# A transformer block pair on one core: the second phase's projections computed as three float32r products in place of one float32 product

## The reference, cut to what matters

```python
def _layer(x, wqkv, qs, ksc, wo, lg, lb, w1, b1, w2, b2):
    h = shift_token(x)                 # half of the channels one token later
    q, k, v = split(h @ wqkv, 3)       # 8 heads of 64
    q = l2norm(q) * qs; k = l2norm(k) * ksc
    q, k = rotary_xpos(q, k)
    o = local_attention(q, k, v)       # windows of 128, own and previous
    x = x + o @ wo
    h = layernorm(shift_token(x)) * lg + lb
    a, g = split(h @ w1 + b1, 2)       # hidden width 682
    return x + (a * gelu(g)) @ w2 + b2
for l in range(2):
    x = _layer(x, wqkv[l], ..., w2[l], b2[l])
return layernorm(x0 + x)
```

## Time and profile before

| | |
|---|---|
| median of three runs | 5642.62 us (5640.09 to 5645.47) |
| the profiled execution, its own time | 5642.98 us |
| its span, first to last instruction | 5641.2 us |
| granted TensorE clock, mean | 0.992 of full speed |
| first phase, about | 0 to 2,700 us |
| second phase, about | 2,700 to 5,641 us |

### The profile page before, as it was taken

The page is one execution under the profiler, slowest core; times in us unless marked ns, Lnnn a source line. Parts: engine busy times, 40 slices in busy tenths (PEclk is TensorE's granted clock), DMA queues, the critical chain, the costliest instruction groups (busy, mean ns, idle before and its releaser), DMA issues.

```text
span 5641.2 us, 145376 instructions
## 1 busy us (share of the span) xinstructions
PE 5465.1 (97%) x57552; PEld 2666.8 (47%) x57552; DVE 4151.5 (74%) x10780; ACT 3453.4 (61%) x6979; POOL 970.1 (17%) x1933
## 2 busy tenths in 40 slices
PE   8999999999999999999799999999999999999998
PEld 3444444444444444533455555555555555555553
DVE  5888888787888888787566667666666777677774
ACT  4766667676666767666455555555556565555654
POOL 2222222232222223222000000000000001010100
PEclk9999999999999999999899999999999999999998
DMA  3333333233333333333100000000000000000000
GB/s 70 55 55 69 55 60 60 50 74 55 66 55 59 63 51 72 55 60 76 43 12 16 8 16 12 12 16 8 16 32 19 16 19 16 20 16 20 19 16 19
DMA packets 128518, 215.60 MB, mean 38 GB/s; under 512 B 40032, under 2 KB 40160, under 8 KB 127072
## 3 DMA queue, kind: packets, MB, share of 16 engines
q1 hardware_dynamic: 127840, 206.30, 18.1%
HBM read 45.73 MB, written 25.17 MB: 13 GB/s over the span
## 4 chain that ended last, share of the span: by engine, by line
PE 71%; ACT 11%; issue 10%; DVE 4%; POOL 3%; SPq 0%; DMA 0%; POOLq 0%; ACTq 0%; DVEq 0%
PE ps L573 22%; PE ps L698 14%; PE ps L819 10%; PE ps L1040 6%; PE ps L1003 5%; PE ps L904 3%; ACT pt L1257 3%; PE ps L896 3%; PE ps L921 3%; ACT gates L1455 1%; ACT sm L1374 1%; PE ps L1005 1%; PE ps L871 1%; PE ps L880 1%; POOL both L2119 1%
## 5 line engine op out<-in xcount | busy, mean ns | idle before, releaser
L1257 ACT ACTIVATE pt<-ps 128x1024 f32<-128x1024 f32 (+7 forms) x2048 | 1237.5, 654 | 616.2 <-PE ps L573 465.1
L698 PE MATMUL ps<-pt,va 128*32 128x512 f32 (+3 forms) x3072 | 1226.5, 487 | 20.0 <-POOL pt L2089 20.0
L698 PE MATMUL ps<-pt,ones 128*32 128x512 f32 (+3 forms) x6144 | 1236.4, 489 | 0.0
L698 PE MATMUL ps<-pt,vs 128*32 128x512 f32 (+3 forms) x3072 | 1230.1, 488 | 0.0
L1631 DVE CUSTOM_DVE_ANT_0 junk<-ps,causal 128x128 bf16<-128x128 f32 (+3 forms) x2048 | 977.8, 487 | 298.4 <-PE ps L573 282.1
L573 PE MATMUL ps<-kt,qt 96*32 96x512 bf16 (+3 forms) x12288 | 1018.6, 329 | 43.8 <-DVE mc L1631 22.7
L573 PE MATMUL ps<-qt,kt 98*32 98x512 bf16 (+3 forms) x12288 | 835.9, 328 | 21.9 <-ACT pt L1257 21.0
L1635 DVE TENSOR_REDUCE mc<-ps 128x1 f32<-128x512 f32 x1024 | 706.4, 690 | 158.7 <-PE ps L573 127.9
L2089 POOL TENSOR_SCALAR_AFFINE_SELECT pt<-pt 128x256 f32<-128x256 f32 x1024 | 466.8, 456 | 1892.2 <-ACT pt L1257 1890.4
L819 PE MATMUL ps<-wqkv,xs 128*128 128x512 f32 x1536 | 727.9, 603 | 0.0
L1374 ACT ACTIVATE sm<-sm,mxw 128x256 f32<-128x256 f32 (+1 forms) x1024 | 493.5, 484 | 241.0 <-DVE mxw L1800 239.6
(11 more groups left out here) (151 smaller groups left out, 8551.3 us busy)
## 6 DMA issues: line engine op xcount, KB each, us to landing
qt<-part SPq DMA_DIRECT2D x768, 64.0 KB, 2.4
kt<-part SPq DMA_DIRECT2D x768, 64.0 KB, 2.5
ya<-wy SPq DMA_DIRECT2D x128, 128.0 KB, 2.3
yb<-wy SPq DMA_DIRECT2D x128, 128.0 KB, 2.3
xs<-between_phases SPq DMA_DIRECT2D x32, 512.0 KB, 3.8
xt<-in_x SPq DMA_DIRECT2D x16, 512.0 KB, 5.6
between_phases<-z SPq DMA_DIRECT2D x16, 512.0 KB, 2.8
between_phases<-xo SPq DMA_DIRECT2D x16, 512.0 KB, 2.7
```

Of the source, the lines that this page charges most:

```text
L698: mmi = pe.matmul(ps[32 * q:32 * q + 32, 4 + half, lo - half * 512:hi - half * 512], w, probs(kb)[:, i, lo - first(kb):hi - first(kb)], st ...
L1257: act.activation(probs(kb)[:, i, kb * P - first(kb):1024 - first(kb)], ps[:, 2 * i:2 * i + 2, :].rearrange("p a q -> p (a q)")[:, kb * P:1 ...
```

## The change

Each float32 matmul of the second phase's projections (`project`, `attention_out`, `gate`, `hidden`, `ffn_out`) becomes three matmuls in the type float32r. For this each operand is split into a rounded part (a copy into a float32r tile) and the residue (operand less rounded part, also float32r): the products are rounded x rounded, rounded x residue and residue x rounded. Scores, transposes, weighing and the means stay float32.

Who splits: VectorE the six gated tiles (`split_hidden`, a copy and a subtraction each) and the first weights and half of x; GpSimd the weights otherwise (`split_w1`, `split_wo`, `split_w2`, `split_wqkv`, once a layer), the inputs (`split_x`, once a half), the heads (`split_heads`, once a window) and the residue of the normalised tile (`residue`, once a half); ScalarE writes the normalised tile's rounded part with one more pass per channel block in `scale_bias`.

To find room, residues lie in place over their operands, `xo` lies over `cn`, the gated tile over `gates`, `sqx` over the rounded gated tile, `ot` is halved to four windows, and sums of squares go in place into `sqf` and `sqx`. There is only one `wqkv` in memory: layer 2's is loaded and split at windows 62 and 63. The residual no longer reads `xs`; SP loads the same data once more into `xm` (`load_residual`).

```diff
+PRODUCTS = (((0, 0, 0, 0), (0, 0, 1, 1), (0, 1, 0, 2)), ((0, 1, 1, 3), (1, 0, 0, 4), (1, 0, 1, 5)))
+THREE = ((0, 0), (1, 0), (0, 1))
...
+            def load_residual(m):
+                lb, half = divmod(m, 2)
+                if m >= 2:
+                    sp.wait_ge(xo_done, done(2 * m - 2))
+                if m:
+                    sp.wait_ge(fc_done, done(2 * m))
+                    sp.wait_ge(xsum_done, done(m))
...
+                load_residual(2 * lb)
...
+                load_residual(2 * lb + 1)
+                if lb + 1 == nb:
+                    sp.wait_ge(qk_full, done(nb * WIN))
+                    fill_qkv(1, 0, 1024)
+                    sp.wait_ge(v_full, done(nb * WIN))
+                    fill_qkv(1, 1024, 1536)
...
-                return pe.matmul(ps[:, bank, :], xs[:, kc, at:at + P], wqkv[l][:, kc, n * 512:n * 512 + 512],
-                                 start=kc == 0, stop=kc == 1)
+                for x, y, kc, k in PRODUCTS[part_of]:
+                    at = w * P + 1 - kc
+                    mmi = pe.matmul(ps[:, bank, :], (xsh, xsl)[x][:, kc, at:at + P], (wh, wl)[y][:, kc, n * 512:n * 512 + 512],
+                                    start=k == 0, stop=k == 5)
...
-                    pe.wait_ge(o_read, done(4 * m + 4))
+                    pe.wait_ge(otl_done, done(4 * m + 4))
...
+            def normed(m, n, to, tile, width, parts):
+                for part_of in parts:
+                    if n == 0 and part_of == 1:
+                        pe.wait_ge(cnl_done, done(2 * m + 2))
+                    for x, y, kc, k in PRODUCTS[part_of]:
+                        mmi = pe.matmul(to, (w1h, w1l)[y][:, kc, tile, 0:width], (cnh, cnl)[x][:, kc, :],
+                                        start=k == 0, stop=k == 5)
...
-                    pe.wait_ge(hn_done, done(2 * m + 2))
+                    pe.wait_ge(cnh_done, done(2 * m + 2))
...
+                    if oc == 0:
+                        pe.wait_ge(hhl_done, done(m * HB + j + 1))
+                    for k, (x, y) in enumerate(THREE):
+                        mmi = pe.matmul(ps[:, fbank(m, 19 + oc), :], (w2h, w2l)[x][rows, j, oc * P:(oc + 1) * P],
+                                        (hhh, hhl)[y][rows, j, :], start=j == 0 and k == 0, stop=j == HB - 1 and k == 2)
...
                 for kc in range(2):
+                    act.activation(cnh[:, kc, :], cn[:, kc, :], ACT.Identity,
+                                   scale=lnp[:, 0, kc:kc + 1], bias=lnp[:, 1, kc:kc + 1]).then_inc(cnh_done, 1)
                     act.activation(cn[:, kc, :], cn[:, kc, :], ACT.Identity,
...
-                dve.tensor_tensor(xm[:, oc, at], ps[:, fbank(m, 1 + oc), :], xs[:, oc, at], ALU.add).then_inc(xm_done, 1)
+                dve.tensor_tensor(xm[:, oc, at], ps[:, fbank(m, 1 + oc), :], xm[:, oc, at], ALU.add).then_inc(xm_done, 1)
...
+            def split_hidden(m, j):
+                dve.wait_ge(hh_done, done(m * HB + j + 1))
+                dve.tensor_copy(hhh[rows, j, :], gb_[rows, j, :]).then_inc(hhh_done, 1)
+                dve.wait_ge(hhh_done, done(m * HB + j + 1))
+                dve.tensor_tensor(hhl[rows, j, :], gb_[rows, j, :], hhh[rows, j, :], ALU.subtract).then_inc(hhl_done, 1)
...
                     gated(m, 1)
+                    split_hidden(m, 0)
                     gated(m, 2)
+                    split_hidden(m, 1)
                     normalise(W, 2)
                     normalise(W, 3)
                     combine(W + 1)
                     gated(m, 3)
+                    split_hidden(m, 2)
                     gated(m, 4)
                     heads_out(W)
+                    split_hidden(m, 3)
                     gated(m, 5)
+                    split_hidden(m, 4)
+                    split_hidden(m, 5)
...
+            def split_heads(W):
+                cols = slice(W % 4 * P, (W % 4 + 1) * P)
+                pool.wait_ge(o_read, done(W + 1))
+                pool.tensor_copy(oth[:, :, cols], ot[:, :, cols]).then_inc(oth_done, 1)
+                pool.wait_ge(oth_done, done(W + 1))
+                pool.tensor_tensor(otl[:, :, cols], ot[:, :, cols], oth[:, :, cols], ALU.subtract).then_inc(otl_done, 1)
...
+                if c == 0:
+                    combine(W + 1)
+                    final_channels(m - 1)
+                    if m >= 0:
+                        sum_channels(m)
+                        sum_squares(m)
+                    split_heads(W)
+                elif c == 1:
+                    residue(m)
+                    combine(W + 1)
+                    split_x(W // WIN + W % WIN // 4, 1 - W % WIN // 4)
+                    final_sum_squares(m - 1)
+                    split_heads(W)
...
+                if W % (4 * FIRST) == 3:
+                    split_wo(W // (4 * FIRST))
+                    split_w1(W // (4 * FIRST))
+                if W % (4 * FIRST) == 6:
+                    split_w2(W // (4 * FIRST))
+                if W == 4 * FIRST - 2:
+                    split_wqkv(1, 0, 1024)
+                if W == 4 * FIRST - 1:
+                    split_wqkv(2, 1024, 1536)
```

More of the change, by code:

```diff
@@ L8 @@
 BF16 = mybir.dt.bfloat16
+F32R = mybir.dt.float32r
 ALU = mybir.AluOpType
@@ L153, in sb, with over @@
             top[0] = at + n
+            place[name] = at
             return nc.alloc_sbuf_tensor_at(name, shape, dt, offset=at)
+        def over(name, other, shape, dt):
+            return nc.alloc_sbuf_tensor_at(name, shape, dt, offset=place[other])
         def sem(name):
@@ L316, in program @@
         stored = [sem(f"stored{h}") for h in range(2)]
-        wq_ready = [sem(f"wq_ready{l}") for l in range(LAYERS)]
+        wq_ready = sem("wq_ready")
         wo_ready = sem("wo_ready")
@@ L953, in mean @@
                 pe.wait_ge(xsum_done, done(m + 1))
-                pe.matmul(ps[:, fbank(m, 3), :], mean_w[:], both[:, 0, :], start=True, stop=True).then_inc(fm_full, 1)
+                pe.matmul(ps[:, fbank(m, 3), :], mean_w[:], both[:], start=True, stop=True).then_inc(fm_full, 1)
             def variance(m):
@@ L961, in variance @@
                 pe.wait_ge(ssum_done, done(m + 1))
-                pe.matmul(ps[:, fbank(m, 4), :], mean_w[:], both[:, 1, :], start=True, stop=True).then_inc(fv_full, 1)
+                pe.matmul(ps[:, fbank(m, 4), :], mean_w[:], sqf[:, 0, :], start=True, stop=True).then_inc(fv_full, 1)
             def final_mean(m, W):
@@ L2134, in final_sum_squares, with split_w1 @@
                 pool.wait_ge(lvar_full, done(n))
-                pool.tensor_tensor(bothf[:, 1, :], sqx[:, 0, :], sqx[:, 1, :], ALU.add).then_inc(lqc_sum, 1)
+                pool.tensor_tensor(sqx[:, 0, :], sqx[:, 0, :], sqx[:, 1, :], ALU.add).then_inc(lqc_sum, 1)
+            def split_w1(l):
+                pool.wait_ge(w1_ready, sent(l + 1))
+                for kc in range(2):
+                    pool.tensor_copy(w1h[:, kc, :, :], w1[:, kc, :, :]).then_inc(w1h_done, 1)
+                for kc in range(2):
+                    pool.wait_ge(w1h_done, done(2 * l + kc + 1))
+                    pool.tensor_tensor(w1l[:, kc, :, :], w1[:, kc, :, :], w1h[:, kc, :, :], ALU.subtract).then_inc(w1l_done, 1)
@@ new lines, in residue @@
+            def residue(m):
+                if m < 0:
+                    return
+                for kc in range(2):
+                    pool.wait_ge(cnh_done, done(2 * m + kc + 1))
+                    pool.wait_ge(hn_done, done(2 * m + kc + 1))
+                    pool.tensor_tensor(cnl[:, kc, :], cn[:, kc, :], cnh[:, kc, :], ALU.subtract).then_inc(cnl_done, 1)
+            def split_heads(W):
[4 more added lines that the diff above has]
+                pool.tensor_tensor(otl[:, :, cols], ot[:, :, cols], oth[:, :, cols], ALU.subtract).then_inc(otl_done, 1)
@@ new lines, in attend @@
+            def attend(W):
+                m, c = half_of(W), W % 4
+                if c == 0:
[11 more added lines that the diff above has]
+                    split_heads(W)
+                elif c == 2:
+                    combine(W + 1)
+                    split_heads(W)
+                else:
+                    combine(W + 1)
+                    split_heads(W)
```

228 lines of the change are left out of this document (148 added, 80 removed).

## The result

The changed kernel takes 5787.69 us (median; 5642.88 before in the same session), a ratio of 1.0258, 95% interval 1.0242 to 1.0274: 144.8 us slower. The profiled execution's span is 5787.4 us. The forecast was 5704 with a range of 5550 to 5830: the sign was right, the size less than half.

A forecast was written before the change was run, and what follows sets the result against it. PE was taken as the bound by a small margin only, over a 71.10 us VectorE and ScalarE loop in each 89.60 us half. The sum was 5643 + 40 (halves) + 21 (once only) = 5704 us, range 5550 to 5830.

The forecast's parts named there:

- The sum's 40 us for the halves: Second phase, collisions included: +0.7 us a half in layer 1, +1.8 in layer 2, 16 halves each.
- 21 once-only us: Layer 2 weight splits (+6, +4.5 each at windows 4 and 68, +5), between phases +3, end -2: +21 us.
- Two signs: Second phase: PE would be below 85% busy and VectorE busier than 80% if the forecast was right.
- The windows without disturbance: Four windows of a half without collisions: c = 0 -1.43, c = 1 -0.9 and +1.15, c = 2 -0.67, c = 3 -2.0 and +2.95.
- the two terms -2.0 and +2.95: Window c = 3: faster PE products save 2.0 us; `largest`, delayed by VectorE's split tail in c = 2, adds 2.95.
- the 1.1 us more for layer 2: Layer 2: VectorE's final add and normalise lie in its loop, no longer covered by PE time; +1.1 us a half.
- a smaller thing is left out of the sum: PE idles some 4 us in c = 3; lower clock for keys and values could cost 1.5 us a half, 48 us.
- Collisions: GpSimd's `split_heads` against VectorE's split tail at the end of c = 2: between 0 and 2.1 us, taken 1.0.
- Collisions everywhere: Rival: 5.1 of GpSimd's 15 us a half obstruct VectorE, in place of 1.6, +3.5 x 32: 5816 us; 14%.
- The tail is swallowed: Rival: VectorE's tail after combine in c = 2 stays within 4.2 us, no collision: 5557 us; 22% up to no change.
- PE stays bound: Rival: PE remains the bound, needing the 71 us loop to shrink by 11: 5190 us; 5%.
- The products are no faster: Rival: float32r products take 0.43 us each, PE becomes the bound with +28.3 us a half: 6549 us; 4%.

The follow-up runs named there:

- experiment 5: On the change: first, unread extra products in c = 1 and c = 3, 5742.6 us; second, these (fewer in c = 3) with GpSimd's c = 2 head split held back, 5695.7 us.
- experiment 6: Against the 5695.7 us kernel: loads and splits of layer 2's four large weights left out, so layer 2 uses layer 1's; 5672.4 us, ratio 1.0055.
- both fillers: The change plus 18 unread products in the wait of c = 3 and four and four in c = 1; 5742.6 us, ratio 1.0179.
- all three edits: The change plus unread products in c = 1 (four and four) and c = 3 (12), and GpSimd's c = 2 head split held back; 5695.7 us, ratio 1.0100.
- experiment 1: The change plus 18 unread key products before TensorE's wait for the maxima in c = 3; 5756.0 us, ratio 1.0202.
- experiments 4, 7 and 8: On the change: VectorE's splits 2 to 5 moved into c = 3, 5726.0 us; ScalarE rounding those tiles, residues and head split moved, 5650.2; last feed-forward product float32, 5621.3.

## Why the prediction was right or wrong

The 144.8 us, as the runs split them, beside the terms of the sum:

| part | measured, us | from | in the sum, us |
|---|---|---|---|
| halves without collision in c = 2 and at full clock | 7 | experiment 5: 16 x 0.2 + 16 x 0.25 | 8 |
| lower clock | 45 | experiment 5, first | 0 (upper end 48) |
| head split beside the tail of c = 2 | 47 | experiment 5, second | 32 |
| layer switch | 23 | experiment 6 | 13 |
| start (windows 0 to 7) and end of the phase | 23 | remainder | 8 |

(The sum's 40 us for the halves held 1.0 x 32 of the tail's collisions; of its 21 once-only us I count 6, 4.5 and 2.5 to the switch.) The edits also change the switch: window 63 takes 32.8 us in the change, 35.9 with both fillers and 38.1 with all three edits. So the parts are good to some 5 us, and the clock and the head split are, if anything, priced too low.

**What bounds the kernel: right.** TensorE became faster and turned that into waiting, first in front of the scores of c = 3 and at the gate, as written. Products at 0.232 us and not 0.215 cost PE 66 x 3 x 0.017 = 3.4 us a half, so it got 10.8 of its 14.2 us; the difference is hidden in those waits. Two signs were set too far: PE is 89% busy (below 85 written), VectorE 76 and 79% (above 80).

**The windows without disturbance: near, and in sum with luck.** c = 0 takes 18.55 us (forecast 18.65), c = 2 21.54 (21.6), c = 1 24.65 where its clock stays up (24.31, or 24.9 with its collision). c = 3 takes 26.08 at full clock and 24.70 without the collision as well (24.14, or 25.15 with a collision of 1.0). The gate's parts began 10.30 and 12.33 us into c = 1 (10.5 and 12.55). The copy of a split took 0.42 us (0.43), its subtraction 0.69; without the collision `largest` comes 7.22 us after `combine` (7.15 written, though the terms listed for it add up to 7.24).

But c = 1 started from 24.06, where 23.78 is typical: it lost 0.87 us, not 0.25, or 0.85 with its collision. c = 3 lost 1.51 (0.95); no run took the lag alone out of it, so how the two terms -2.0 and +2.95 share that miss is open. And the 1.1 us more for layer 2 did not come. Without the tail's collision the sum had -0.3 us a half in layer 1 and +0.8 in layer 2; measured are +0.2 and +0.25. That 7 us stand beside 8 is two errors of 8 and 9 us which cancel.

**The step that failed** is the last one, "a smaller thing is left out of the sum". Its working was right: PE idles in c = 3, keys and values run at the lower level, up to 1.5 us a half, 48 us; measured 45. That the two are so near is partly chance: c = 3 lost 1.8 us in layer 1 and 1.4 in layer 2 (experiment 1), and it was not only c = 3, since behind the two waits at the gate, 1.03 and 1.09 us, c = 1 lost 1.1 us too in every second half of layer 1. Nothing in the rows spoke for leaving it out, and the earlier trace rows showed the fall after 2.00 idle us, while the forecast itself had PE idle for 4. It belonged in the sum: 5704 + 48 = 5752. What is left to 5788 comes from two terms of the wrong size, which follow.

**Collisions were mis-sized.** In the tail of c = 2: 1.0 taken between bounds of 0 and 2.1, 47 / 32 = 1.5 measured (in the trace 0.3 in a subtraction and 1.1 in the product, which holds as few as 42 partitions and yet ends only 0.55 us after GpSimd's 128-row subtraction). The Trainium skill's page "SBUF — State Buffer" (section SBUF: two separate sides) has the loser of the shared ports wait for the winner's whole instruction, and counts VectorE's two-port copies. The trace agrees for both: 1.76 us for the product beside 1.60 of GpSimd, and 3.63 for a copy that takes 0.41 elsewhere.

**Once-only terms were too small**, 46 us for 21. Read from the windows of the change against others of their kind: `split_wo` and `split_w1` in front of GpSimd's part of `combine` make windows 4 and 68 longer by 7.3 and 7.5 us (25.82 for 18.56 and 27.03 for 19.56; 4.5 each counted). `split_w2`, whose subtraction holds up the copy shown above, makes the wait in front of the scores of c = 3 8.85 us in place of 4.48 and windows 7 and 71 some 4.1 us longer (2.5 each counted):

```profile
4304.50 1.13 PE L963 MATMUL ps<-kp,qp 64*128 64x256 f32 x8
...
4331.53 1.13 PE L963 MATMUL ps<-kp,qp 64*128 64x256 f32 x8
...
4390.36 2.08 PE L963 MATMUL ps<-kp,qp 64*128 64x256 f32 x8 [8.85 <-DVE mxw L1889]
```

Queries of window 64 wait 9.60 us, half of it in place of the usual wait of window 63: windows 63 and 64 are 5.0 and 2.4 us longer (6 counted). From the first scores of the last window to the end it takes 102.3 us in place of 96.0, 6 more where 2 fewer were counted. No run took the 23 us of start and end apart; in the kernel with all three edits 13 of them lie in windows 4 to 7 (102.4 us for 89.3) and 6 behind the last scores.

**The rivals.** "Collisions everywhere" (5816) came nearest in size, by the wrong way: they cost 47 us in one place, not 5.1 us a half. "The tail is swallowed" and "PE stays bound" needed a tail within 4.2 us and a shorter loop; experiments 4, 7 and 8 have that tail only with splits moved out of it or left out. "The products are no faster" is refuted by the pitch.

## What to carry to other kernels

When an engine that was the bound is made faster, price what its new waits do to its clock: here each wait of 1 to 4.5 us could be paid a second time, at half speed, by the work behind it. Convert the parts of the work whose extra operations fall on idle engines, and leave the one whose operations fall on the loop: four of five projections in float32r gained 0.35% (0.55% with the gate tiles interleaved), while all five lost 2.6% as first placed and came out within 0.2% of the kernel before (5643 to 5650 us) once the splits were placed on idle engines. Keep GpSimd's two-input operations away from a tail on VectorE: here one collision cost a product of 42 rows 1.1 us, more than it takes alone.

## What was not expected of the hardware

Useless work made the kernel faster: up to 26 products a half that nobody reads, 45 us less. The lower level came after waits of TensorE as short as 1.03 and 1.09 us with 0.9 us of work between them, though only in every second half, and its low stretches in one window grew or shrank (3.4 or 6.8 us) with edits in another.
